# Row sums of the x1 stage issued five tiles behind their mix on TensorE instead of eight

## What is computed

```python
# layer 0: a 1x1 mix of the channels, leaky ReLU, scaled by its own minimum and maximum
y = einsum('bchw,oc->bohw', gn(x), W2) + b[0]
y = where(y >= 0, y, 0.1 * y)
x1 = x + (y - min_hw(y)) / (max_hw(y) - min_hw(y) + 1e-8)
# layer 1: a 3x3 convolution of the 2-d real Fourier spectrum of gn(x1), complex weights, and back
X = rfftn(gn(x1));  Y = conv3x3(X, w_real + i*w_imag) + bias;  x2 = x1 + irfftn(Y)
# layers 2 and 3: two more 3x3 convolutions (one quantised, one circular)
```

## Time and profile before

| what | value |
|---|---|
| median of 3 runs | 6585.06 us (6578.19 to 6588.43) |
| the profiled execution: its own time | 6585.46 us |
| its span, first to last instruction | 6583.6 us |
| mean granted TensorE clock | 0.955 of full speed |
| busy share of the span | PE 87%, PEld 56%, DVE 75%, ACT 69%, POOL 41% |
| PE, mix matmuls (`pM<-X,mix0s`, line 272) | 2304 records, 633 ns each |
| PE, row-sum matmuls (`pP<-X,sumw`, line 272) | 2048 records, 589 ns each |

### The profile page before, as it was taken

The page is one execution under the profiler, slowest core; times in us unless marked ns, Lnnn a source line. Parts: engine busy times, 40 slices in busy tenths (PEclk is TensorE's granted clock), DMA queues, the critical chain, the costliest instruction groups (busy, mean ns, idle before and its releaser), DMA issues. The chain is left out here.

```text
span 6583.6 us, 201217 instructions
## 1 busy us (share of the span) xinstructions
PE 5696.3 (87%) x64138; PEld 3661.9 (56%) x64138; DVE 4922.5 (75%) x9721; ACT 4531.8 (69%) x8793; POOL 2724.0 (41%) x4633
## 2 busy tenths in 40 slices
PE   0389979979979989989988988994989889889889
PEld 0058748748848757756766766771433334334334
DVE  5778877877887887887887887887767667667664
ACT  2577767767767766766766547556878778778776
POOL 2165556556556555556546546550111111111111
PEclk9899989989999999999999999997999999999999
DMA  6426616615625634643642541552767667667665
GB/s 182 169 59 185 186 41 187 185 54 177 185 75 157 185 99 133 184 124 105 185 145 67 142 130 48 143 141 43 196 168 198 167 167 203 163 170 202 169 172 137
DMA packets 535623, 959.19 MB, mean 146 GB/s; under 512 B 121946, under 2 KB 126682, under 8 KB 532826
## 3 DMA queue, kind: packets, MB, share of 16 engines
q1 hardware_dynamic: 467546, 799.21, 43.9%
q10 hardware_dynamic: 67456, 151.01, 7.1%
HBM read 560.66 MB, written 287.60 MB: 129 GB/s over the span
## 5 line engine op out<-in xcount | busy, mean ns | idle before, releaser
L1613 PE MATMUL pC<-xs,taps 128*128 128x512 f16 x4608 | 1094.3, 382 | 105.9 <-DMA xhalo<-xs 101.4
L966 PE MATMUL pM<-gw,xh 64*128 64x256 f16 (+1 forms) x24960 | 1128.7, 244 | 0.0
L966 PEld LDWEIGHTS pM<-gw,xh 64*128 64x128 f16 x24960 | 966.8, 95 | 129.7 <-issue 3.3
L728 POOL TENSOR_TENSOR X<-X,zo 128x256 f32 (+1 forms) x512 | 371.5, 726 | 1244.1 <-DVE X L1077 1244.1
L1613 PEld LDWEIGHTS pC<-xs,taps 128*128 128x128 f16 x4608 | 448.8, 98 | 668.8 <-DVE xs L1662 88.3
L1509 POOL TENSOR_TENSOR xn<-xn,one_col 128x1 f32<-128x1 f32 x520 | 159.4, 307 | 1401.0 <-ACT xn L1543 1401.0
L1529 ACT ACTIVATE scaled<-X,qbias,qscale 128x512 f32 (+1 forms) x512 | 411.0, 804 | 344.9 <-DMA X<-after_layer 284.7
L272 PE MATMUL pM<-X,mix0s 64*64 64x512 f32 x2304 | 528.4, 633 | 133.9 <-DVE X L1049 108.3
L1077 DVE SCALAR_TENSOR_TENSOR X<-pZ,X 128x512 f32 (+1 forms) x512 | 353.8, 691 | 327.3 <-ACT zo L787 326.1
L1551 ACT ACTIVATE xs<-xn 128x1028 f16<-128x1028 f32 x520 | 545.7, 1049 | 73.5 <-POOL xn L1510 72.2
L713 POOL TENSOR_TENSOR X<-X,rl 128x512 f32 x384 | 478.2, 1275 | 269.4 <-ACT rl L758 269.0
(11 more groups left out here) (241 smaller groups left out, 13755.0 us busy)
## 6 DMA issues: line engine op xcount, KB each, us to landing
gw<-row_weights SPq DMA_DIRECT2D x520, 288.0 KB, 3.1
after_layer<-X SPq DMA_DIRECT2D x512, 256.0 KB
out_dram<-result SPq DMA_DIRECT2D x512, 256.0 KB
X<-in_x_dram SPq DMA_DIRECT2D x448, 256.0 KB
X<-after_layer ACTq DMA_DIRECT2D x224, 512.0 KB, 5.8
stage<-in_x_dram SPq DMA_DIRECT2D x192, 512.0 KB
xhalo<-xs SPq DMA_DIRECT2D x504, 96.4 KB, 3.7
qhalo<-q SPq DMA_DIRECT2D x496, 96.2 KB, 4.0
```

The costliest lines, as they stand in the source:

```text
L728: nc.gpsimd.tensor_tensor(X[:, j, 0], X[:, j, 0], zo[:, k], ALU.add)
L966: nc.tensor.matmul(pY[:, r, col:col + nd * P], row(xh, r)[:, k, p, ri, off:off + P], weights(r, q_, d, nd, ri), start=ri == 0 and off == 1 ...
L1613: nc.tensor.matmul(bank, taps3[:, d, wh], xs[:, h, own, d:d + W], start=d == 0 and n == 0, stop=False)
```

## The change

After the change `row_sums` follows the mix by five tiles instead of eight. Row sums begin behind mix 5 instead of mix 8: mix 5 is followed by the row sums of tile 0, mix 63 by those of tile 58, and behind the last mix stand five row sums (tiles 59 to 63) instead of eight. No instruction is added or removed. Every row sum keeps its own wait; which mix it stands behind changes, and so the group of the tile: behind the mixes k = 0, 1, 2, 3 now stand the row sums of tiles k = 3 (two groups back), 0, 1 and 2 (one group back), where before stood those of k = 0, 1, 2, 3 (two groups back).

```diff
                         for j in range(J):
                             mix(b, j)
-                            if j >= 8:
-                                row_sums(b, j - 8)
-                        for j in range(J - 8, J):
+                            if j >= 5:
+                                row_sums(b, j - 5)
+                        for j in range(J - 5, J):
                             row_sums(b, j)
                         pe.wait_ge(rows_ready, b + 1)
```

## The result

| | before | after |
|---|---|---|
| median | 6586.75 us (8 runs, 6578.19 to 6600.64) | 6555.14 us (8 runs, 6539.31 to 6566.10) |
| ratio | | 0.9951, 95% interval 0.9937 to 0.9964 |
| span of the profiled execution | 6583.6 us | 6553.3 us |
| mean granted clock | 0.955 | 0.958 |

The change saves 0.49% (0.36 to 0.63%), some 32 us, where 13 were forecast. It is faster by more than the bound of 0.2%, and its median lies 9 us under the lower end of the range.

The account below looks back on a forecast made before the run. DVE was taken to pace mid-stage, and the row sums' chain to delay the Fourier stage at the x1 stage's end. 11.4 + 2.2 - 0.4 = 13.2 us off the median 6585.06 gave 6572 us, range 6564 to 6582.

Parts of the forecast that it names:

- Step 1: End of the x1 stage: three tiles' row sums leave it, so row sums end 2.1 us earlier, not 2.58.
- Step 2: Closing: line 1170 starts 1.42 us earlier per image, 11.4 us in eight; DVE's own statistics are late next.
- Step 3: Small matmuls in the closing: DVE's wait falls from 1.02 to 0.75 us, 2.2 us gained in eight images.
- Step 4: Mid-stage x1: row sums now wait for younger tiles, some 0.1 us, covered by PE's 0.96 us; cost nothing.
- Step 5: Start of the x1 stage: row sums between mixes 5 to 8 cost at most 0.05 us, 0.4 in eight images.
- Rival B: Start of the x1 stage: strict PE order makes mixes wait for row sums, 4.8 us lost, 6576.7; chance 0.08.
- Rows 2: Profile timeline of one mid-stage group, read as a matmul for a free quarter overtaking one whose quarter is busy.
- rival A: Fourier stage start: PE's clock returns at its own time, half the gain lost, 6.6 us gained, 6578.5; chance 0.10.

Follow-up runs that it names:

- e7: Row sums four tiles behind the mix, against five in the changed kernel: 6566.10 us, ratio 0.9978 to the kernel before.
- e8: Row sums three tiles behind the mix, against five in the changed kernel: 6602.09 us, ratio 1.0036 to the kernel before.
- e1: Changed kernel (lag five) plus seven short DVE copies before line 1170: 6579.94 us, ratio 0.9987 to the kernel before.
- e11: Changed kernel (lag five) plus three short DVE copies before line 1170: 6564.00 us, ratio 0.9972 to the kernel before.
- e2: Kernel before (lag eight) with row sums of tiles 56 to 58 left out, output not the reference's: 6556.74 us, ratio 0.9970.
- e3: Kernel before (lag eight) plus 27 idle matmuls on PE before the Fourier stage's first transpose: 6555.41 us, ratio 0.9962.

## Why the prediction was wrong

Step 1 held. The row sums end at about 405.13 with ACT starting at 405.17, 1.19 us before line 1167 starts; before it was 0.83 us after it (410.91 against 410.08). That is 2.0 us gained on this pair, 2.1 forecast; tile 61 waited 0.15 us for POOL's second addition (399.69 + 2.50 = 402.19).

Step 2 held: DVE's own statistics are next, line 1170 starts 0.19 us after line 1167 instead of 1.62, 1.43 us gained, 1.42 forecast.

Step 3 held: the wait at line 242 is 0.70 us, 0.75 forecast, so 0.32 us gained instead of 0.27. Together 1.75 in image 0's rows and 1.74 in the mean, 13.9 us in eight images.

Step 4 held: mid-stage cost nothing, 0.2 of 0.97 us of cover were used. e7 and e8 show where the cover ends: with lag four the x1 stage is some 0.5 us longer at an equal return of the clock, with lag three 4.6.

Step 5 was priced at 0.05 us per image; the x1 stage is 0.32 us longer. It is not the row sum in front of mix 7: DVE's waits at line 1043 are 3.9 us in 8 times instead of 1.6 in 3, up to 1.0 us each, but in e1, which has lag five too, they are 1.5 in 3 and the stage is 77.46 us. In the two traces the stage takes 77.8 to 78.2 us in the images where the clock reaches full speed over 1.5 us after line 1148 (two before, four after), and 76.8 to 77.6 in the others. The stage's first mixes run at half speed, and the longer they do, the later DVE gets them. Rival B, strict order on PE, had no part: it would have shown as DVE waits of 0.4 us in every image, those of e1 too.

Rows 2 show less than the prediction read from them. Only a pass overtakes: as whole matmuls the mix goes from 349.56 to 350.63 and the row sum issued behind it from 349.71 to 350.78, so both starts and ends are in the order of issue. Whether the two passes of one matmul are instructions of their own the trace does not tell. The rows therefore do not speak against an order by whole matmuls, and what they do show is that a row sum on free quarters does not hold the mix beside it for the length of its passes.

**What failed is the term that was not in the sum**: I let the Fourier stage keep its length and treated the clock only as rival A, with one sign. Half of the time at half speed is lost, as rival A has it (four us cost two), and the return does not simply move with the work. But it did not stay at its own time either: it came 4 to 5 us sooner relative to the work, which is a gain. I gave the loss 0.10 and the gain nothing, beside the words "it can also fall luckily". It fell so in eight images of eight; nothing in the change aims at it, so this part of the gain is luck. The difference of the means is 1.95 us per image, and the wait at line 1127 has no part in it: what it has above 0.68 us is 0.54 us per image before (2.73 and 2.41 in two of seven) and 0.53 after (2.40, 1.12 and 2.25 in three). Eight times 2 us are 16. With that term, known only now, the forecast would have been 6572 - 16 = 6556, and 6555.14 was measured. Turning the sign of rival A as it was priced (6.6 us) would not have done: with the spread of the runs that reaches down to 6560. Its size was too small as well, 0.8 us per image where 2 came.

The profile before had a sign of it, though not the size. Its images differ: the clock came back 14.2 to 14.5 us after line 770 in six and 14.9 to 15.1 in two, though line 770 follows the last tile by the same 8.2 us in each. A return that does not keep its distance to the work is one to be priced on both sides when the work is moved by 1.7 us.

## What to carry to other kernels

When a change moves a stage's start by a microsecond or two and PE's clock is at half speed there, the clock's return need not move along: here it came 4 to 5 us earlier or as late as before. Price it with both signs, and split a measured gain by stages before the change is given credit for all of it; here about half was the clock's, and 1.3 us of delay in another place took it away again. Where PE is idle for some microseconds in a serial stretch between two full stages, idle matmuls in the gap (their number fitted to the wait) are worth trying: here they gave another 0.5% at no cost on the path. A lag between producer and consumer on one queue should be just long enough that the wait is over or hidden behind another one; a further step is paid at the stage's end once nothing else is later there (the sixth cost 0.1 us, the seventh and each after it 0.8 to 0.9).

## What had not been expected of the hardware

The lengths of one and the same stage fall into two groups, 428.2 and 430.2 us in the middle, with the clock's return at 8.4 to 10.3 or 14.1 to 15.3 us after the start and nothing between, and neighbouring images of one execution may be in different groups (e11: 428.2 and 430.4 us). Which group dominates changes with the time from image to image: all early for closings of 6.5 to 6.6 us (lags five and six, e2), all but one late for 7.8 (e1), all late for 8.2 (before), mixed at 7.04 and 7.46, two early at 11.7, but also mixed for lag four at 6.48 with an x1 stage longer by 0.3 us, and six late for lag three at 6.48. So the length of the closing alone does not say it, and what sets the moments of the clock's changes was not tried.

At the change of image PE starts its first small matmul up to 3 us after DVE has its operand ready, with an idle time that the profile puts down to nothing ("issue"); in one execution some images have this delay and some not (line 1127 above). The loop over the images closes on PE's queue at that place, and the traces point at the loading of its code. They list the packets of an instruction queue (q8) among the DMAs: in 23 of the 26 images with a wait above 0.68 us such a packet lands 1.65 to 1.71 us before the first small matmul starts, as if the matmul had waited for it, while in the images with a wait of 0.68 us the last one before the matmul lands 2.3 to 3.1 us ahead. No run tests this.

Outside these stages the traces scatter more than the change is worth: from line 770 of the last image to the end it took 2535.7 (e3) to 2564.2 us (e11) in kernels that have the same instructions there, which is why single spans were not used as verdicts.
